# Weighing V in plain fp32 with V stationary in four groups of 32 columns

## The reference

```python
q, v, k = (qvk[:, :, 0], qvk[:, :, 1], qvk[:, :, 2])
scores = jnp.einsum('bshi,bthi->bsth', q, k)
scores = (scores + mask[None, :, :, None]) / math.sqrt(d)     # causal
weights = jax.nn.softmax(scores, axis=2)
wv = jnp.einsum('bsth,bthi->bshi', weights, v).reshape(b, s, d)
return wv @ Wo
...
x = x + _layernorm(attention(_layernorm(x)))
x = x + _layernorm(ffn(_layernorm(x)))
```

## Time and profile before

| | us |
|---|---|
| median of two runs | 3904.6 (3904.42 to 3904.77) |
| span of the profiled execution | 3921.7 |
| projection, to the first matmul of attention | 623.1 |
| start of attention (first unit's maxima) | 25.9 |
| attention's slots, to the end of the last Wo | 1751.5 |
| feed-forward | 1521.2 |

### The profile page before, as it was taken

How to read it: one execution, slowest core, us unless ns; L and a number is a source line. 1 busy time by engine, 2 the same in 40 slices (tenths; PEclk the granted TensorE clock), 3 DMA queues, 4 the chain that set the end, 5 groups by cost and what they waited for, 6 DMA issues and landing times. The chain is left out here.

```text
span 3921.7 us, 71979 instructions
## 1 busy us (share of the span) xinstructions
PE 3633.4 (93%) x26145; PEld 3017.0 (77%) x26145; DVE 2510.8 (64%) x4546; ACT 2075.8 (53%) x2708; POOL 1627.6 (42%) x1213
## 2 busy tenths in 40 slices
PE   7999995999989998999999994999999999999998
PEld 6888873787777777777777874788888888888886
DVE  4444434877777777877778775566666666666665
ACT  2222221867667676767668684444444444444443
POOL 2233332878778787878778884000000000000000
PEclk9999995999898989999899997999999999999999
DMA  4555544334243333433343324000001000000000
GB/s 178 210 204 189 189 180 109 83 79 109 71 113 88 84 92 97 104 78 99 78 109 97 104 56 148 1 23 22 22 22 40 26 22 22 23 22 22 22 22 22
DMA packets 183098, 321.82 MB, mean 82 GB/s; under 512 B 13136, under 2 KB 48016, under 8 KB 182288
## 3 DMA queue, kind: packets, MB, share of 16 engines
q1 hardware_dynamic: 182800, 317.54, 27.5%
HBM read 189.83 MB, written 126.62 MB: 81 GB/s over the span
## 5 line engine op out<-in xcount | busy, mean ns | idle before, releaser
L899 POOL TENSOR_TENSOR a_prob_lo<-a_prob,a_prob_hi 128x1024 f16<-128x1024 f32 (+1 forms) x640 | 1246.8, 1963 | 393.9 <-ACT a_prob_hi L788 392.2
L816 DVE TENSOR_REDUCE a_mx<-a_pw 128x1 f32<-128x512 f32 (+3 forms) x1216 | 782.5, 659 | 277.9 <-PE a_pw L674 187.8
L781 ACT ACTIVATE a_prob<-a_pst,a_lift 128x1024 f32<-128x1024 f32 (+1 forms) x640 | 656.2, 1025 | 470.0 <-PE a_pst L723 252.1
L1288 PE MATMUL f_py<-f_w,f_act 128*128 128x512 f32 x3072 | 749.5, 394 | 5.4 <-DVE f_act L1156 3.5
L1278 PE MATMUL f_ph<-f_xT,f_w 128*128 128x512 f32 x3072 | 736.2, 390 | 6.3 <-issue 4.9
L719 PE MATMUL a_pst<-a_qp,a_kp 98*128 98x256 f32 x2560 | 692.4, 345 | 27.0 <-ACT a_prob L781 16.3
L671 PE MATMUL a_pw<-a_kp,a_qp 96*128 96x512 f32 (+3 forms) x1536 | 620.0, 429 | 87.6 <-DVE a_mx L816 44.1
L1278 PEld LDWEIGHTS f_ph<-f_xT,f_w 128*128 128x128 f32 x3072 | 577.8, 188 | 129.3 <-issue 7.4
L1288 PEld LDWEIGHTS f_py<-f_w,f_act 128*128 128x128 f32 x3072 | 568.5, 188 | 138.6 <-DVE f_act L1156 18.0
L788 ACT ACTIVATE a_prob_hi<-a_prob 128x1024 f16<-128x1024 f32 (+1 forms) x640 | 616.5, 963 | 0.0
L1093 POOL TENSOR_TENSOR f_ve<-f_mv,f_eps 128x4 f32<-128x4 f32 x32 | 7.7, 241 | 1452.9 <-DVE f_mv L1114 1452.9
(11 more groups left out here) (126 smaller groups left out, 4337.1 us busy)
## 6 DMA issues: line engine op xcount, KB each, us to landing
qk_parts<-q_stage SPq DMA_DIRECT2D x128, 512.0 KB, 3.7
a_qp<-qk_parts SPq DMA_DIRECT2D x192, 256.0 KB, 4.7
a_kp<-qk_parts SPq DMA_DIRECT2D x192, 256.0 KB, 5.8
v_parts<-q_vstage SPq DMA_DIRECT2D x16, 1584.0 KB, 6.5
a_vt<-v_parts SPq DMA_DIRECT2D x32, 792.0 KB, 7.2
q_x<-in_L_attn_h_dram SPq DMA_DIRECT2D x16, 1024.0 KB, 9.4
a_xr<-in_L_attn_h_dram SPq DMA_DIRECT2D x64, 256.0 KB, 3.5
x<-a_y SPq DMA_DIRECT2D x64, 256.0 KB, 2.5
```

The costliest lines, as they stand in the source:

```text
L781: act.activation(prob[:, k % PR, :, off:QC], pst[:, k % 2, :, off:QC], ACT.Exp, scale=SCALE, bias=lift[:, :]).then_inc(exp_done, 1)
L816: dve.tensor_reduce(out, src, AX_X, ALU.max).then_inc(released, 1)
L899: pool.tensor_tensor(prob_lo[:, k % HR, :, off:QC], prob[:, k % PR, :, off:QC], prob_hi[:, k % HR, :, off:QC], ALU.subtract).then_inc(lo_d ...
L1288: last = pe.matmul(py[:, t, :], act_r[:, f % AR, b, t * P:(t + 1) * P], w2s[:, a, f, :], start=(f == 0 and j == 0), stop=(f == NF - 1 and ...
```

## The change

V is stored and loaded as one fp32 tensor (`v_parts` rows of 544 fp32, of which 512 are used; `vt` 128 x 8 x 128 fp32 for each of two buffers). The fp16 copy, its rest and the three parts of V are gone, and with them the work of ACT at L788, of POOL at L899, L203 and L206, and of DVE at L262. In `weigh` the roles turn round: the stationary operand is V of one head, 128 keys x 32 columns, the moving one is `prob` in plain fp32, up to 256 queries wide, and the four heads write four different groups of 32 output partitions of one PSUM bank. A second set of four matmuls has a stationary block of ones (128 x 32) and writes the denominators, repeated over 32 partitions, to a second bank. The output comes out transposed already, so the turns go. DVE takes the reciprocal of a whole 128 x 256 block out of PSUM, multiplies, and splits into `oT` from SBUF. LAG is 3 instead of 6, `prob` has 7 buffers instead of 5.

```diff
-        vt = sb("vt", [P, 2, QT, HPG * VH], BF16)
+        vt = sb("vt", [P, 2, QT, P])
+        ones = sb("ones", [P, HD])
...
-                    first = first_query(k) // P
-                    if t < first:
-                        return
-                    if t == first:
-                        pe.wait_ge(lo_done, NS * v + k + 1)
+                    off = first_query(k)
+                    if t == 0:
+                        pe.wait_ge(exp_done, NS * v + k + 1)
                         if k == 0:
                             pe.wait_ge(v_loaded[b], 16 * (2 * i + u // 2 + 1))
-                    if j == 0:
-                        wait(pe, acc_read, TQ * (NC * v + c - 1) + t + 1)
+                        if j == 0:
+                            wait(pe, acc_read, NC * v + c)
                     for h in range(HPG):
-                        for part, skip in ((prob_hi, 0), (prob_lo, VF)):
-                            last = pe.matmul(acc[:, t, h * VH + skip:(h + 1) * VH],
-                                             part[:, k % HR, h, t * P:(t + 1) * P],
-                                             vt[:, b, j, h * VH:(h + 1) * VH - skip],
-                                             start=(j == 0 and h == 0 and not skip),
-                                             stop=(j == TQ * c + t and h == HPG - 1 and skip > 0))
+                        rows = slice(h * HD, (h + 1) * HD)
+                        last = pe.matmul(acc[rows, t, off:QC], vt[:, b, j, rows] if t == 0 else ones[:, :],
+                                         prob[:, k % PR, h, off:QC], start=(j == 0), stop=(j == TQ * c + TQ - 1))
...
                 def normalise(i, u, c):
                     n = NC * (UNITS * i + u) + c
-                    dve.wait_ge(acc_read, TQ * (n + 1))
-                    dve.reciprocal(rden[:, :, :], osum[:, :, :, HD]).then_inc(rden_done, 1)
+                    cols = slice(c * QC, (c + 1) * QC)
+                    dve.wait_ge(pv_done, NS * (UNITS * i + u) + LAST_OF_C[c] + 1)
+                    dve.reciprocal(rden[:, :], acc[:, 1, 0:QC]).then_inc(rden_done, 1)
                     dve.wait_ge(rden_done, n + 1)
-                    dve.tensor_tensor(o[:, c % 2].rearrange("p t (h f) -> p t h f", f=HD), osum[:, :, :, 0:HD],
-                                      rden[:, :, :].unsqueeze(3).to_broadcast([P, TQ, HPG, HD]), ALU.mult
-                                      ).then_inc(o_done, 1)
+                    dve.tensor_tensor(o[:, :], acc[:, 0, 0:QC], rden[:, :], ALU.mult).then_inc(acc_read, 1)
+                    dve.wait_ge(acc_read, n + 1)
+                    dve.tensor_copy(oT[:, 0, u % UNITS, cols], o[:, :]).then_inc(oT_hi, 1)
+                    dve.wait_ge(oT_hi, n + 1)
+                    dve.tensor_tensor(oT[:, 1, u % UNITS, cols], o[:, :], oT[:, 0, u % UNITS, cols].bitcast(F32),
+                                      ALU.subtract).then_inc(o_done, 1)
```

More of the change, by code:

```diff
@@ L329, in output @@
                     else:
-                        pe.wait_ge(v_rest, TPC * n + before + MM - QK + 1)
+                        pe.wait_ge(v_out, TPC * n + before + MM - QK - TPC + 1 + TPC)
                     if m == 0:
@@ L383, in score_pieces @@
     return out
-LAG = 6
-TURN_AT = [k + LAG + 2 for k in LAST_OF_C]
+LAG = 3
 PIECES = score_pieces()
@@ L444, in shared_work @@
                     out.append((u, k, "max", u + 1, 0))
-            for c, at in enumerate(TURN_AT):
-                e = self.earlier(u, k, at)
-                if e and e[1] == 0:
-                    out.append((u, k, "turn", e[0], c))
             out += [(u, k, "wo", b, m) for b, m in self.halves(u, k, 0)]
@@ L597, in _ @@
                 pool.memset(half[:, :], -0.5)
+                pool.memset(ones[:, :], 1.0)
                 pool.memset(eps[:, :], EPS)
@@ L691, in shared @@
                                             ident[:, :])
-                    elif what == "turn":
-                        pe.wait_ge(o_done, NC * (UNITS * i + unit) + m + 1)
-                        for t in range(TQ):
-                            last = pe.transpose(pw[:, bank, t * P:(t + 1) * P], o[:, m % 2, t, :], ident[:, :])
                     else:
                         if m % (2 * TQ) == 0:
-                            turn = next((n for n, it in enumerate(stage.work)
-                                         if it[2:] == ("turn", UNITS * unit + UNITS - 1, m // (2 * TQ))), 0)
-                            pe.wait_ge(released, before + turn + 1)
+                            pe.wait_ge(o_done, NC * (UNITS * (i + unit) + UNITS - 1) + m // (2 * TQ) + 1)
                         terms = [(g, a, w) for g in range(GROUPS) for w, a in PASSES]
@@ L778, in exponentials @@
                     v, off = UNITS * i + u, first_query(k)
-                    wait(act, lo_done, NS * v + k - PR + 1)
+                    wait(act, pv_done, NS * v + k - PR + 1)
                     act.wait_ge(st_done, NS * v + k + 1)
@@ L782, in exponentials @@
                                    bias=lift[:, :]).then_inc(exp_done, 1)
-                def high(i, u, k):
-                    v, off = UNITS * i + u, first_query(k)
-                    act.wait_ge(exp_done, NS * v + k + 1)
-                    wait(act, pv_done, NS * v + k - HR + 1)
-                    act.activation(prob_hi[:, k % HR, :, off:QC], prob[:, k % PR, :, off:QC], ACT.Copy
-                                   ).then_inc(hi_done, 1)
                 def wo_norm(i, t):
@@ L828, in maxima @@
                                                  ALU.subtract).then_inc(released, 1)
-                def sums(i, u, c, t):
-                    dve.wait_ge(pv_done, NS * (UNITS * i + u) + STEPS.index((c, TQ * c + t)) + 1)
-                    if t == 0:
-                        wait(dve, o_done, NC * (UNITS * i + u) + c)
-                    dve.tensor_reduce(osum[:, t], acc[:, t, 0:HPG * VH].rearrange("p (h a f) -> p h f a", a=VP, f=VF),
-                                      AX_X, ALU.add).then_inc(acc_read, 1)
@@ L869, in shared @@
                     bank = ((before if isinstance(before, int) else work_before(0, stage)) + at) % 2
-                    if what == "turn":
-                        turned(i, unit, m, at, before, bank)
-                    elif what == "wo":
+                    if what == "wo":
                         wo_stats(i + unit, m, at, before, bank)
@@ L882, in run @@
                         e = stage.earlier(u, k, LAG)
-                        if e:
-                            c, j = STEPS[e[1]]
-                            if j >= TQ * c:
-                                sums(i, e[0], c, j - TQ * c)
-                            if e[1] in LAST_OF_C:
-                                normalise(i, e[0], c)
+                        if e and e[1] in LAST_OF_C:
+                            normalise(i, e[0], STEPS[e[1]][0])
                 for at, (what, m) in enumerate(AHEAD):
```

76 lines of the change are left out of this document (14 added, 62 removed).

## The result

The changed kernel takes **4371.7 us** (two runs, 4367.8 to 4375.6) against 3904.6: 1.1215 times as long, with a 95% interval of 1.1182 to 1.1248. It is slower by 12%, where 18% was forecast; the time lies between the likeliest case (4612) and the rival with four heads side by side (4215), nearer to the rival.

The account below looks back on a forecast made before the run. PE's instruction stream was taken to bound the kernel. From the 3921.7 us span, -6 - 364 + 1042 + 205 - 100 - 70 gave 4629, less 17 for timed runs 4612 us, 18% slower; range 4090 to 5720.

Parts of the forecast that it names:

- the likeliest case: Weighing on PE: heads' matmuls overlap two at a time, four passes each; 4612 us, chance 0.37.
- the rival with four heads side by side: Weighing on PE: all four column groups stream at once, 521 us of weighing; 4215 us, chance 0.24.
- Slower by over 2%: Whole kernel: the forecast sign, slower by more than the 2% a measurement can tell; chance 0.90.
- Weighing, +1042 us: PE in attention's slots: 4608 fp32 streams of 256 columns, four passes of 113 ns, two heads at a time.
- The change of width, nothing: PE between full-width and 32-column matmuls: no cost added; a drain of 0.17 us would have made it 220 us higher.
- The reciprocal's wait, +205 us: End of each query block: PE waits for DVE's reciprocal and multiply, 1.6 us, 128 times.
- Waits regained, -100 us: PE's waits for DVE in attention's slots, 110 us in all: 100 us come back with DVE freed.
- Clock regained, -70 us: Attention's slots: half of what the lower clock costs comes back, since PE stands still for a smaller share.
- The projection, -6 us: Projection's end: V is stored without two POOL steps, 6 us off, between 3 and 10.
- What goes, -364 us: PE's stream in attention's slots: the old weighing matmuls, 346 us, and the turns, 18 us, disappear.
- the cheap reciprocal with all waits regained: Variant of the likeliest forecast: reciprocal at its lower bound and all of PE's waits regained; 4370 us.
- one after another: Weighing on PE: no heads overlap, 2083 us of weighing; 5613 us, chance 0.26.

Follow-up runs that it names:

- one_group: Changed kernel, but after each block's first step all four heads write the same 32 output partitions (output not the reference's); 5410.5 us.
- joined: Changed kernel with the V and ones matmuls back to back in every slot, no shared work between them; 4297.2 us.
- pairs: Changed kernel weighing two steps in every even slot, V and V, then ones and ones; 4447.2 us.
- full_width: Changed kernel with 128-column stationary blocks of V or ones, all heads on the same 128 partitions (output not the reference's); 5380.5 us.
- split: Changed kernel with half of a step's scores put between the V and ones matmuls in every slot; 5083.3 us.
- few_ones: Changed kernel without the ones matmuls except in each block's last step and a unit's first block (denominators not the reference's); 4429.2 us.
- filler: few_ones with two needless one-pass full-width matmuls of 128 x 256 in place of each ones set left out; 4164.4 us.
- pool_sum: Changed kernel with GpSimd adding up a block's probabilities, PE multiplying only that sum by ones, except in a unit's first block; 4688.4 us.
- copy_out: Changed kernel with ACT copying V's sums and DVE the denominators to SBUF at a block's end, reciprocal taken from there; 4504.5 us.

## Why the prediction was right, and where it was not

Slower by over 2% was right, and for the reason given: PE sets the pace, the work taken from ACT and POOL lay beside it (the slots' PE share is 0.92 before and 0.91 after), and weighing in plain fp32 holds PE longer than the sixteen short matmuls did. That the time came within 6% of 4612 was luck, as the steps show:

- **Weighing, +1042 us.** The step that failed. It took two heads at a time, from the reading that PE starts in program order and that only neighbours overlap. one_group showed four side by side; the term is 524 us, where the rival had 521. Four passes and 113 ns a pass were right.
- **The change of width, nothing.** Wrong, by the choice of a row. The earlier trace rows shows the scores 40 ns behind a transpose onto 32 columns, and I let it stand for all. In that row PE had stood idle for 0.26 us ahead of the transpose, so nothing could be seen on the way in; and in one_group, where nothing waits, the same transpose (L655) pays no change in either direction, in 31 of its 32 cases:

```profile
732.98 0.51 PE L678 MATMUL a_pst<-a_qp,a_kp 98*128 98x256 f32 x2
733.32 0.27 PE L655 MATMUL a_pw<-a_ident,a_mx 128*32 128x128 f32 x1
733.35 0.48 PE L678 MATMUL a_pst<-a_qp,a_kp 98*128 98x256 f32 x2
```

  A transpose is no measure for the weighing then; what sets it apart was not tried. By the rest, joined, pairs and full_width give 0.23, 0.21 and 0.25 us for a change there and back. At 865 of them that is 180 to 220 us. The Trainium skill, TensorEngine Tiling (Array Packing), Tiling Modes, says that a change of mode drains TensorE; the runs agree that it costs, and the +220 us that the prediction worked out from 0.17 us twice in 640 slots was near.
- **The reciprocal's wait, +205 us.** Mis-sized: 138 us. The reciprocal took 1744 ns and not 2.1 us, which is 46 of the 67 us; the multiply's 425 ns was right, and the other 21 us were not taken apart. The sentence on the maxima queued behind it was right too, and matters more than I had made of it: it is why taking the wait away gives 10 us.
- **Waits regained, -100 us.** The maximum L760 fell to 175 ns as said, so GpSimd had held it. PE's waits for maxima of before, 110 us, are 46 now: 64 us regained.
- **Clock regained, -70 us.** Wrong in sign. The idea was that PE stands still for a smaller share of the time and so keeps its clock. It went from 0.92 to 0.90 over a longer stretch, which by the table costs 96 us more.
- **The projection, -6 us,** was -4; feed-forward stayed within 7 us, as the premise asked.
- **What goes, -364 us.** Too small, by one slot standing for all. By the starts in the trace of before, taken as for split, the weighing holds PE for 384 us (39 ns a start and not 37.5, and it begins 27 ns later behind a mask matmul than the scores do) and the turns for 25: 409 us. The line at its way in, beside 1504.04 in the earlier trace rows:

```profile
1503.97 0.23 PE L674 MATMUL a_pw<-a_mask_q,a_identb 128*128 128x128 bf16 x1
```

The same count gives 708 us for the changed kernel: 524 of streaming and 184 around it, 0.21 us for each of the 862 visits that the trace holds. So PE's stream grew by 299 us, where the rest in the table grew by 276.

In sum, on the span: -4 + 708 - 409 + 138 - 64 + 96 + 7 = +472, against +452 measured; the 20 us between them stay open. The forecast of 4612 took weighing 518 us too dear and width and clock 350 us too cheap (184 and 166), and these partly cancelled. The 4370 us that the prediction names for the cheap reciprocal with all waits regained is 4397 by its own terms, and neither condition came, so that it is close to the 4371.7 measured says nothing. The range held the result because it reached from four side by side to one after another.

## What to carry to other kernels

Four products of 32 output columns in plain fp32 cost TensorE as much as one, but each visit to that layout costs another 0.2 to 0.3 us, so collect the visits. A wait for an engine is worth removing only if that engine has time before the next wait for it; else look at its longest run (here the division of 256 columns on VectorE; shortening it was not tried). And read the granted clock before crediting work taken from TensorE: here leaving out 218 us of it gained nothing, and putting back some 115 us of another kind gained 265.

## What the runs showed of the hardware

- **The granted clock doesn't follow PE's busy share.** In few_ones PE is busy for 95% of the slots and gets 0.67 (0.69 to 0.72 by the estimate for its other executions); in full_width for 95% and gets 0.99; in filler for 92% and gets 0.89. Low were the kernels in which short sets onto 32 columns stand alone among one-pass matmuls at full width (few_ones 0.67, pool_sum 0.69, split 0.67); high were those with long plain fp32 stretches (one_group 0.96, full_width 0.99). The order of the matmuls alone doesn't settle it either: copy_out has the changed kernel's, and gets 0.85 instead of 0.90. At 1.2 GHz a V set ahead of a return to full width takes 1.01 us to the next start instead of 0.57. What in such a set lowers the clock was not taken apart, and stays open.
- A plain fp32 matmul leaves two records and costs four passes of 109 to 114 ns for 256 columns. The change from full width to 32 columns and back costs 0.21 to 0.26 us (joined, split, pairs, full_width), and nothing around the transpose onto 32 columns (one_group, full_width).
- A reciprocal of 256 fp32 columns on VectorE takes 1744 ns from PSUM, 6.8 ns a column, and 1753 from SBUF (copy_out); eight columns took 204.
- A small VectorE instruction on SBUF can take as long as the GpSimd instruction beside it: 175, 1595 and 2304 ns for the same 16 columns, with GpSimd idle, at 2161 and at 2372 ns.
